# FFN weights laid out transposed by the host and made ternary in pieces of 512 columns; small inputs in one transfer

## The chip, the cores and the metric

The kernel runs on one NeuronCore of a Trainium2 chip, as one launch. The metric is device time in microseconds (us). Engines are TensorE (PE), VectorE (DVE), ScalarE (ACT), GpSimd (POOL) and SyncE (SP), which here issues all transfers. Each engine works off its own instructions in the order in which they are written; semaphores hold them to each other.

## What is computed

For 16 batches of 256 tokens of 512 elements: a gated attention (mLSTM, 8 heads of 64) on a layer norm of x with a context, then a gated FFN with quantised activations and ternary weights.

```python
def weight_quant(w):
    scale = 1.0 / jnp.clip(jnp.mean(jnp.abs(w)), EPS, None)
    q = jnp.clip(jnp.round(w * scale), -1.0, 1.0) / scale
    return w + jax.lax.stop_gradient(q - w)
def bitlinear(x, w):
    return act_quant(x) @ weight_quant(w).T
g = bitlinear(x, w_gate)                 # w_gate, w_up: (2048, 512)
u = bitlinear(x, w_up)
h = jnp.square(jax.nn.relu(g)) * u
return bitlinear(h, w_down)              # w_down: (512, 2048)
...
x = x + jnp.tanh(g_xattn[0]) * _L0_xattn_ref(_layernorm(x), ctx_1024, ctx_1024, ...)
x = x + jnp.tanh(g_ffn[0]) * _L0_ffn_ref(_layernorm(x), w_gate, w_up, w_down)
```

A weight becomes -1, 0 or 1 after division by the mean magnitude of its whole matrix; the mean must be known before any of it can be used.

## The kernel before

Tokens lie on the 128 partitions, two tiles (t = 0, 1) for a batch. `schedule` calls, on every engine, `step(b, n, m, par)`: the FFN of batch b, the attention of batch n and the preparation of batch m (layer norm, transposes, gates) in one hand-written order, with b = n - 1 and m = n + 1. The first calls are `step(None, None, 0, 0)`, `step(None, 0, 1, 1)` and `step(0, 1, 2, 0)`, which the code calls `first`, `second` and `third`; then a loop, and three closing steps.

Within a step TensorE multiplies the FFN's hidden layer in chunks of 512 columns (`chunk`, L1002, banks `gb` and `ub`), computes head scores (`scores`, L1033 and L1034), head outputs (`heads_out`, L1044 to L1046), gate products (`gate_products`, L1085), exponents (`exponents`, L1053) and the down projection (`down`, L1023). ScalarE takes the exponentials (L470, L471), relu and square (L435, L437), copies head outputs from the bank `tp` (`heads`, L479), and computes `lz` and `rz` (L557, L559), from which VectorE's `scale_heads` and the residual `x2` follow; GpSimd adds the second half, `x2[1]` (L395). `quantise_tokens` needs both. `gates_in` (L719) comes after it on VectorE, `running_max` (L739 to L750) gives `mparts`, which the next step's exponents need.

The weights are made ready in the first three steps. SyncE loads each in four pieces of 1 MB into `stage[0]` (gate, down) and `stage[1]` (up). `magnitudes(m, i)` sums absolute values (VectorE L618, ScalarE L415), `weight_total` adds them over partitions on TensorE (L974), and `weight_scale` makes mean and inverse (L608 to L613). Then, for each piece of 2048 elements a partition: `scale_weight` multiplies by the inverse and adds the magic number 12582912, which rounds (GpSimd L363, ScalarE L421); `round_weight` subtracts it into `rounded` in bf16 (VectorE L627, ScalarE L428); `weight_columns` transposes 16 blocks on TensorE into the banks `gb` and `ub` (L985); `weight_cols` copies two banks to `wgT`, `wuT` or `wdT` and clips to -1 and 1 (VectorE L642). The first `chunk` waits for all 24 banks (`wt_free`).

Eight small transfers bring gate kernels, biases and the two gates' scalars (`small_in`); ScalarE's first instruction and GpSimd's sum into `gk` (L357) wait for all of them. GpSimd builds constants first, `pick` among them (L351). `rounded`, `relu`, `h`, `ot`, `hqT` and `hq` share space: `relu` and `hq` lie in the `stage` tiles.

## Time and profile before

| | |
|---|---|
| median of 3 runs | 747.88 us (747.65 to 748.24) |
| span of the profiled execution | 748.3 us |
| TensorE busy | 676.4 us (90%) |
| VectorE busy | 604.8 us (81%) |
| ScalarE busy | 438.8 us (59%) |
| GpSimd busy | 122.7 us (16%) |
| memory traffic | 29.48 MB read, 8.39 MB written |
| chain that ended last | PE 60%, DVE 21%, issue 10%, ACT 6% |

In a table of stages the columns are the stage, its length, busy us of PE, PE weight load, DVE, ACT and POOL (with instructions), the granted clock, the DMA share and GB/s. A group by line ends in busy us, mean ns of one, and idle us before it. Times in a row count from the start of the span. "Idle before" names the time for which an engine had nothing running ahead of a group, and what ended it. The granted clock is given as a share of full speed: 1.00 is 2.4 GHz, 0.50 is 1.2 GHz.

### The profile page before, as it was taken

What the parts mean: (1) busy time and instruction counts of PE and PEld (TensorE: products, weight loads), DVE (VectorE), ACT (ScalarE), POOL (GpSimd) and SP (SyncE); (2) the same over time, 40 slices, a digit from 0 to 9 for tenths busy, and PEclk for the clock granted to TensorE, in tenths of its full rate; (3) what the DMA queues carried; (4) which work ended last, traced back from release to release, by engine and by line L of the source; (5) the groups of instructions that cost most, each with busy time, mean ns of one, the idle gap of its engine ahead of it and who ended that gap; (6) DMA issues with size and microseconds to landing.
All of it is one profiled execution on the core that took longest, in us unless ns stands there. A gap on an engine that the chain in (4) does not pass through costs nothing.

```text
span 748.3 us, 14597 instructions
## 1 busy us (share of the span) xinstructions
PE 676.4 (90%) x4634; PEld 460.8 (62%) x4710; DVE 604.8 (81%) x1374; ACT 438.8 (59%) x945; POOL 122.7 (16%) x188
## 2 busy tenths in 40 slices
PE   2778499999989999899989999899989999999896
PEld 2568467574756666575756666575757666675543
DVE  2585879797987979797987979797978979797966
ACT  2697556657574646656574646556574646566542
POOL 3341120202010110202020210202020200202000
PEclk9986699999999999999999999999999999999989
DMA  6950100102020201002020202002010102000000
GB/s 197 392 204 1 57 1 18 69 1 71 15 72 14 70 14 52 34 0 71 14 71 14 70 14 70 15 0 74 10 71 14 70 14 71 15 15 16 1 29 28
DMA packets 22132, 38.42 MB, mean 51 GB/s; under 512 B 5184, under 2 KB 5184, under 8 KB 21568
## 3 DMA queue, kind: packets, MB, share of 16 engines
q1 hardware_dynamic: 22080, 37.87, 14.2%
q14 instruction: 37, 0.30, 0.1%
q8 instruction: 15, 0.25, 0.1%
HBM read 29.48 MB, written 8.39 MB: 51 GB/s over the span
## 4 chain that ended last, share of the span: by engine, by line
PE 60%; DVE 21%; issue 10%; ACT 6%; DVEq 1%; DMA 1%; SPq 1%; POOL 0%; ACTq 0%
PE yb L1023 11%; PE ub L1002 11%; PE gb L1002 10%; PE ab L1033 5%; DVE hmaxes L657 4%; PE ab L1013 3%; PE tp L1044 3%; PE tp L1085 3%; PE tp L1046 2%; PE tp L1045 2%; PE ab L1053 2%; DVE dmat L763 2%; DVE stage L649 2%; PE ab L1034 2%; PE ab L1063 2%
## 5 line engine op out<-in xcount | busy, mean ns | idle before, releaser
L1002 PE MATMUL ub<-wuT,xqT 128*128 128x512 bf16 x497 | 131.7, 381 | 8.9 <-DVE stage L649 8.0
L1023 PE MATMUL yb<-wdT,stage 128*128 128x512 bf16 x483 | 133.6, 379 | 1.3 <-ACT stage L449 0.5
L1002 PE MATMUL gb<-wgT,xqT 128*128 128x512 bf16 x480 | 126.4, 383 | 5.9 <-ACT xqT L456 4.2
L479 ACT ACTIVATE ysb<-tp 128x260 f32<-128x260 f32 x64 | 24.7, 387 | 149.8 <-PE tp L1046 149.8
L379 POOL TENSOR_SCALAR_AFFINE_SELECT dmat<-dmat 128x256 f32<-128x256 f32 x128 | 61.8, 510 | 238.5 <-ACT dmat L471 238.3
L649 DVE TENSOR_TENSOR stage<-stage,ub 128x512 f32<-128x512 f32 x128 | 86.7, 680 | 16.5 <-ACT stage L437 16.5
L763 DVE SCALAR_TENSOR_TENSOR dmat<-ab,dmat 128x384 f32<-128x384 f32 x128 | 65.3, 551 | 40.0 <-PE ab L1034 39.3
L1002 PEld LDWEIGHTS ub<-wuT,xqT 128*128 128x128 bf16 x512 | 49.0, 98 | 68.2 <-DVE stage L649 9.8
L435 ACT ACTIVATE stage<-gb 128x512 f32<-128x512 f32 x128 | 76.5, 598 | 20.2 <-PE gb L1002 15.8
L437 ACT ACTIVATE stage<-stage 128x512 f32<-128x512 f32 x128 | 80.7, 630 | 4.1
L1023 PEld LDWEIGHTS yb<-wdT,stage 128*128 128x128 bf16 x512 | 59.3, 118 | 38.1 <-DVE stage L696 0.7
L657 DVE TENSOR_REDUCE hmaxes<-stage 128x1 f32<-128x1536 f32 (+1 forms) x64 | 77.6, 1213 | 0.6
L395 POOL TENSOR_TENSOR x<-ysq,xs 128x512 f32<-128x512 f32 x16 | 25.3, 1582 | 309.6 <-DVE ysq L796 309.6
L1002 PEld LDWEIGHTS gb<-wgT,xqT 128*128 128x128 bf16 x512 | 47.5, 101 | 44.7 <-issue 8.1
L470 ACT ACTIVATE dmat<-ab,a 128x256 f32<-128x256 f32 x128 | 62.3, 487 | 1.0 <-PE ab L1053 1.0
L1033 PE MATMUL ab<-qT,cT 64*128 64x256 f32 x256 | 55.0, 441 | 5.3 <-DVE dmat L763 5.2
L1044 PE MATMUL tp<-values,dmat 128*128 128x65 f32 x256 | 51.9, 285 | 5.7 <-issue 5.7
L1045 PE MATMUL tp<-values,dmat 128*128 128x65 f32 x256 | 50.5, 279 | 0.0
L1046 PE MATMUL tp<-values,dmat 128*128 128x65 f32 x256 | 50.5, 280 | 0.0
L471 ACT ACTIVATE dmat<-ab,a 128x128 f32<-128x128 f32 x128 | 49.6, 387 | 0.0
L679 DVE TENSOR_SCALAR stage<-stage,hqs 128x1024 f16<-128x1024 f32 x64 | 47.4, 783 | 2.4 <-DVE hqs L671 1.5
L1044 PEld LDWEIGHTS tp<-values,dmat 128*128 128x128 f32 x256 | 40.7, 194 | 13.6 <-issue 6.0
(134 smaller groups left out, 1198.4 us busy)
## 6 DMA issues: line engine op xcount, KB each, us to landing
xs<-in_x SPq DMA_DIRECT2D x16, 512.0 KB, 3.6
cx<-in_ctx SPq DMA_DIRECT2D x16, 512.0 KB, 4.4
out<-stage SPq DMA_DIRECT2D x32, 256.0 KB, 2.0
stage<-in_L_ffn_w_gate SPq DMA_DIRECT2D x4, 1024.0 KB, 11.1
stage<-in_L_ffn_w_up SPq DMA_DIRECT2D x4, 1024.0 KB, 13.9
stage<-in_L_ffn_w_down SPq DMA_DIRECT2D x4, 1024.0 KB, 5.4
gk<-in_L_xattn_igate_kernel SPq DMA_DIRECT2D x1, 48.0 KB, 4.4
gk<-in_L_xattn_fgate_kernel SPq DMA_DIRECT2D x1, 48.0 KB, 4.5
```

What stands on the lines that cost most here:

```text
L435: nc.scalar.activation(relu[:, c % 2, :], gb[c % 2][:, :], ACT.Relu).then_inc(g_free, 1)
L437: nc.scalar.activation(relu[:, c % 2, :], relu[:, c % 2, :], ACT.Square).then_inc(r2_ready, 1)
L470: nc.scalar.activation(dmat[:, hd, 0:2, :].rearrange("p c s -> p (c s)"), eb, ACT.Exp, bias=a[npar][:, 0, hd:hd + 1])
L649: nc.vector.tensor_tensor(h[t][:, c * CH:(c + 1) * CH], relu[:, c % 2, :], ub[c % 2][:, :], ALU.mult).then_inc(h_done, 1)
L657: nc.vector.tensor_reduce(hmaxes[:, t, part:part + 1], h[t][:, first * CH:last * CH], axis=AX_X, op=ALU.max, apply_absolute_value=True).th ...
L763: nc.vector.scalar_tensor_tensor(dh, ab[hd % 2][:, 0:3 * P], HD ** -0.5, dh, ALU.mult, ALU.mult).then_inc(a_free[hd % 2], 1)
L1002: last = nc.tensor.matmul(bank[c % 2][:, :], xqT[par][:, t, d, :], w[:, d, c * CH:(c + 1) * CH], start=(d == 0), stop=(d == KD - 1))
L1023: done = nc.tensor.matmul(yb[:, :], hqT[:, c, :], wdT[:, c, :], start=(c == 0), stop=(c == KF - 1))
L1033: nc.tensor.matmul(ab[e][:, 0:S], cT[npar][rows, kd, 0:P], qT[npar][rows, kd, 0:S], start=True, stop=True)
L1044: nc.tensor.matmul(o0, dmat[:, hd, 0, :], values[:, 0, hd, :], start=True, stop=True)
L1045: nc.tensor.matmul(o1, dmat[:, hd, 1, :], values[:, 0, hd, :], start=True, stop=False)
L1046: last = nc.tensor.matmul(o1, dmat[:, hd, 2, :], values[:, 1, hd, :], start=False, stop=True)
```

## The change

The host hands over `w_gate`, `w_up` and `w_down` transposed, so that they land in `stage` in the layout that the matmuls read, and packs gate kernels, biases and both scalars, the latter repeated for each partition, into one array of 128 x 226 floats. `weight_columns` (192 transposes), VectorE's `weight_cols` and the tiles `rounded` and `identb` go. A piece is now 512 columns of all four row blocks (gate, up) or four row blocks (down). After scaling with the magic number, gate and down pieces become ternary by ScalarE's Sign of the value less the magic number (`sign_weight`), up pieces by VectorE's subtract and max, then min (`round_weight`). The matmuls wait for the piece that they read (`w_ready`). `relu` and `hq` get tiles of their own. The work on `w_down` after its transfer (magnitudes, total, scaling, signs) moves from the second step to the third; `w_down`'s transfers wait for the signs of the gate pieces whose place they take. The order of other steps in `second` changes too: ScalarE takes all four exponentials at once, and batch 1's statistics and norm come after `normaliser`.

```diff
...
+        def weight_piece(m, i):
+            return stage[m % 2][:, PW * i:PW * (i + 1)]
+        def ternary_piece(m, i):
+            if m == 2:
+                return wdT[:, KD * i:KD * (i + 1), :]
+            return (wgT, wuT)[m][:, :, CH * i:CH * (i + 1)]
+        def by_rows(piece):
+            return piece.rearrange("p (k c) -> p k c", k=KD)
...
+            sp.dma_start(small[:, :], small_in).then_inc(small_ready, 16)
             sp.dma_start(xs[0][:, :, :], x[0].rearrange("(t p) d -> p t d", p=P)).then_inc(x_in[0], 16)
             sp.dma_start(cx[0][:, :, :], ctx_in[0].rearrange("(t p) d -> p t d", p=P)).then_inc(c_in[0], 16)
-            for i, (kern, bias) in enumerate(((wi, bi), (wf, bf))):
-                sp.dma_start(gk[:, :, i * NH:(i + 1) * NH], kern.rearrange("(c p) h -> p c h", p=P)).then_inc(small_in, 16)
...
-            def weights(m, w):
...
+            def weights(m, w, first, last):
+                wv = w.rearrange("(k p) f -> p k f", p=P)
+                for i in range(first, last):
                     if m == 2:
-                        sp.wait_ge(w_round[i % 2], i // 2 + 1)
-                    sp.dma_start(sv[:, rows * i:rows * (i + 1), :], wv[:, rows * i:rows * (i + 1), :]).then_inc(w_in[m][i], 16)
+                        sp.wait_ge(w_ready[0], i + 1)
+                        src = wv[:, KD * i:KD * (i + 1), :]
+                    else:
+                        src = wv[:, :, CH * i:CH * (i + 1)]
+                    sp.dma_start(by_rows(weight_piece(m, i)), src).then_inc(w_in[m][i], 16)
...
-            weights(0, w_gate)
+            weights(0, w_gate, 0, 4)
+            weights(1, w_up, 0, 2)
             load(1, 1)
-            weights(1, w_up)
-            weights(2, w_down)
+            weights(1, w_up, 2, 4)
+            weights(2, w_down, 0, 4)
...
                     gp.wait_ge(a_free[p % 2], exponent_use(n, p // 2) + 1)
...
+                    if b is None:
+                        scale_weight(0, p)
+                if at(b, 0):
+                    scale_weight(2, 0)
+                    scale_weight(2, 1)
                 if b is None:
                     scale_weight(1, 0)
-                    scale_weight(1, 2)
+                    scale_weight(1, 1)
...
                 if b is None:
-                    scale_weight(2, 0)
-                    scale_weight(2, 2)
+                    scale_weight(1, 2)
+                    scale_weight(1, 3)
...
-                nc.scalar.activation(x2[1][:, :, :].rearrange("p t d -> p (t d)").bitcast(BF16), stage[m % 2][:, PW * i:PW * (i + 1)],
-                                     ACT.Abs, accum_out=asum[:, m, i:i + 1]).then_inc(asum_done[1], 1)
+                nc.scalar.activation(wdT[:, 0:KD, :], by_rows(weight_piece(m, i)), ACT.Abs, accum_out=asum[:, m, i:i + 1]).then_inc(asum_done[1], 1)
...
+            def sign_weight(m, i, scaled):
+                act.wait_ge(w_scaled[m], scaled)
+                nc.scalar.activation(ternary_piece(m, i), by_rows(weight_piece(m, i)), ACT.Sign,
+                                     bias=minus_magic[:, :]).then_inc(w_ready[m], 1)
...
-                if third:
-                    round_weight(2, 3)
-                elif b is not None:
+                if b is not None and not third:
                     relu_square(b, 0, 0)
                 if n is not None:
                     exponentials(n, 0, npar)
                     exponentials(n, 1, npar)
-                if second:
...
-                if third:
+                if third or second:
                     exponentials(n, 2, npar)
                     exponentials(n, 3, npar)
+                if third:
                     relu_square(b, 0, 0)
                 if b is not None:
                     relu_square(b, 0, 1)
+                if third:
+                    magnitudes(2, 0, 4)
...
                     relu_square(b, 0, 2)
-                if n is not None and not third:
+                if third:
+                    magnitudes(2, 1, 5)
...
                 if second:
-                    scale_weight(0, 3)
-                    for i in range(4):
-                        magnitudes(1, i)
+                    sign_weight(0, 0, 1)
+                    magnitudes(1, 0, 2)
                 if first:
                     act.wait_ge(consts, 3)
-                if m is not None:
+                if m is not None and not second:
...
                     exp_minus_max(n, npar)
                     heads(n, 0)
-                if second:
-                    for i in range(4):
-                        magnitudes(2, i)
                 if b is not None:
                     relu_square(b, 0, 3)
+                if third:
+                    magnitudes(2, 2, 6)
+                    magnitudes(2, 3, 7)
...
                 if n is not None:
                     heads(n, 1)
                     if second:
-                        scale_weight(1, 1)
-                        round_weight(1, 1)
+                        sign_weight(0, 1, 2)
...
+                if third:
+                    scale_weight(2, 2)
+                    scale_weight(2, 3)
+                    sign_weight(2, 0, 4)
+                    sign_weight(2, 1, 4)
                 if b is not None:
                     relu_square(b, 1, 1)
                     hidden_cols(b, 0)
+                if third:
+                    sign_weight(2, 2, 4)
+                    sign_weight(2, 3, 4)
                 if second:
-                    for t in range(T):
-                        columns(m, 0, cT[par], t)
-                    scale_weight(1, 3)
+                    magnitudes(1, 2, 3)
+                    act.wait_ge(stat_step, STAT_K * m + 4)
+                    rstd_of(mv[:, :, 1], lnv[:, :], rstd[:, :], rstd_step, RSTD_K * m)
...
-                if m is not None and not second:
+                if second:
+                    sign_weight(0, 2, 3)
+                if m is not None:
...
+                if first:
+                    magnitudes(0, 2, 0)
                 if second:
-                    scale_weight(2, 3)
-                if first:
-                    magnitudes(0, 2)
-                    magnitudes(0, 3)
+                    sign_weight(0, 3, 4)
                 if n is not None:
                     tokens(n, npar)
-                if second:
-                    round_weight(2, 1)
...
+                if first:
+                    magnitudes(0, 3, 1)
...
+            def round_weight(i):
+                dve.wait_ge(w_scaled[1], i + 1)
+                nc.vector.tensor_scalar(ternary_piece(1, i), by_rows(weight_piece(1, i)), MAGIC32, -1.0,
+                                        ALU.subtract, ALU.max).then_inc(w_low, 1)
+                dve.wait_ge(w_low, i + 1)
+                nc.vector.tensor_scalar(ternary_piece(1, i), ternary_piece(1, i), 1.0, None, ALU.min).then_inc(w_ready[1], 1)
...
-                if m is not None:
+                if m is not None and not second:
                     attention_stats(m, par)
...
-                if second:
-                    round_weight(0, 0)
-                    round_weight(0, 1)
-                    weight_cols(0, 0)
...
                     if second:
-                        weight_cols(0, 2)
-                if m is not None:
+                        magnitudes(1, 1)
+                if m is not None and not second:
                     attention_norm(m, par)
...
+                if first:
+                    magnitudes(0, 0)
...
+                if n is not None:
+                    weigh(n, 6)
+                    weigh(n, 7)
+                    if at(b, 0):
+                        weight_scale(2)
+                        dve.wait_ge(winv_step, WINV[2])
+                        dve.wait_ge(tanh_done, 1)
+                        nc.vector.scalar_tensor_tensor(wprod[:, 2:3], wmean[:, 2:3], 1.0 / 127.0, tanhs[:, 1:2],
+                                                       ALU.mult, ALU.mult).then_inc(winv_step, 1)
+                if b is not None:
+                    quantise_hidden(b, 0, par)
+                    hidden(b, 1, 0)
+                if n is not None:
+                    normaliser(n, npar)
                 if second:
-                    weight_cols(0, 3)
+                    attention_stats(m, par)
+                    magnitudes(1, 3)
+                    attention_norm(m, par)
+                if b is not None:
+                    hidden_cols(b, 0)
...
+                if n is not None:
+                    if at(n, 0):
+                        dve.wait_ge(tanh_done, 1)
+                    scale_heads(n)
+                    residual(n, npar)
+                if second:
                     weight_scale(1)
                     dve.wait_ge(winv_step, WINV[1])
...
-                    normaliser(n, npar)
...
-                    weight_cols(1, 1)
-                    weight_scale(2)
...
+                if second:
+                    round_weight(0)
                 if m is not None:
-                    if second:
-                        weight_cols(1, 2)
                     log_forget(m)
                 if second:
-                    round_weight(2, 0)
+                    round_weight(1)
...
                 if first:
+                    magnitudes(0, 1)
                     weight_scale(0)
                 if second:
-                    weight_cols(1, 3)
-                    weight_cols(2, 0)
-                    round_weight(2, 2)
-                    weight_cols(2, 1)
-                    weight_cols(2, 2)
-                    weight_cols(2, 3)
+                    round_weight(2)
+                    round_weight(3)
...
-                pe.wait_ge(asum_done[1], 4 * m + 2)
+                pe.wait_ge(asum_done[0], (2, 4, 4)[m])
+                pe.wait_ge(asum_done[1], (2, 4, 8)[m])
...
-            def weight_columns(m, i, between=None):
...
-                        last = nc.tensor.transpose(wt_bank(g)[:, s * P:(s + 1) * P], rounded[:, i % 2, piece * P:(piece + 1) * P], identb[:, :])
...
+                for bank, w, full, free, ready in ((gb, wgT, g_full, g_free, w_ready[0]), (ub, wuT, u_full, h_done, w_ready[1]))[first:last]:
                     if at(b, 0) and t == 0:
-                        pe.wait_ge(wt_free, 24)
-                for bank, w, full, free in ((gb, wgT, g_full, g_free), (ub, wuT, u_full, h_done))[first:last]:
+                        pe.wait_ge(ready, c + 1)
...
+                    if at(b, 0) and t == 0 and c % KD == 0:
+                        pe.wait_ge(w_ready[2], c // KD + 1)
                     done = nc.tensor.matmul(yb[:, :], hqT[:, c, :], wdT[:, c, :], start=(c == 0), stop=(c == KF - 1))
...
                 if third:
-                    weight_columns(2, 2)
-                    weight_columns(2, 3)
                     exponents(n, 2, npar)
...
                     heads_out(n, 3, npar)
                 if second:
-                    weight_columns(1, 1)
+                    weight_total(1)
+                if third:
                     weight_total(2)
...
                 if first:
                     weight_total(0)
-                if second:
-                    weight_columns(1, 3)
-                    weight_columns(2, 0)
-                    weight_columns(2, 1)
...
+    laid = {name: np.asarray(a) for name, a in inputs.items()}
+    heads = laid["L0_xattn_igate_bias"].shape[0]
+    kernels = np.concatenate([laid["L0_xattn_igate_kernel"], laid["L0_xattn_fgate_kernel"]], axis=1)
+    kernels = kernels.reshape(-1, P, 2 * heads).transpose(1, 0, 2).reshape(P, -1)
+    biases = np.concatenate([laid["L0_xattn_igate_bias"], laid["L0_xattn_fgate_bias"]] * 2
+                            + [laid["g_xattn"], laid["g_ffn"]]).reshape(1, -1)
+    laid["small"] = np.concatenate([kernels, np.broadcast_to(biases, (P, biases.shape[1]))], axis=1)
+    for name in ("w_gate", "w_up", "w_down"):
+        laid[name] = laid["L0_ffn_" + name].T
...
```

## Rows read from the trace of the kernel before

**Rows 1.** Busy time by stage: window, each engine's busy us, clock, DMA.

```profile
100.00:120.00 20.00, 19.26 (x136) 13.93 (x137) 17.30 (x40) 9.87 (x22) 0.00 (x0) 1.00 0.00 1
...
131.20:172.00 40.80, 39.82 (x277) 26.94 (x282) 35.05 (x83) 24.26 (x57) 6.41 (x10) 1.00 0.10 36
```

**Rows 2.** Timelines of ScalarE: first exponential of batches 0, 1 and 2.

```profile
30.92 0.47 ACT L470 ACTIVATE dmat<-ab,a 128x256 f32<-128x256 f32 x1 [1.02 <-PE ab L1053]
...
92.83 0.46 ACT L470 ACTIVATE dmat<-ab,a 128x256 f32<-128x256 f32 x1
...
134.08 0.46 ACT L470 ACTIVATE dmat<-ab,a 128x256 f32<-128x256 f32 x1
```

**Rows 3.** Timeline of all engines, 0 to 24 us.

```profile
4.10 3.55 POOL L351 TENSOR_SCALAR_AFFINE_SELECT pick<-pick 72x1024 bf16<-72x1024 bf16 x3
...
12.93 0.20 ACT L406 ACTIVATE tanhs<-tanhs 128x2 f32<-128x2 f32 x1 [10.84 <-DMA tanhs<-in_g_ffn]
...
13.15 1.28 ACT L407 ACT_TABLE_LOAD   x1
...
15.60 1.86 PE L1085 MATMUL tp<-gk,cT 128*128 128x16 f32 x8 [8.01 <-ACT cT L441]
...
15.93 2.28 DVE L618 TENSOR_REDUCE asum<-stage 128x1 f32<-128x2048 f32 x1
```

**Rows 4.** Timeline, 22 to 60 us: gates, and the maximum's last part.

```profile
24.43 0.19 DVE L719 TENSOR_TENSOR gates<-tp,gbias 128x32 f32<-128x32 f32 x1 [3.75 <-PE tp L1085]
...
29.80 0.42 DVE L750 TENSOR_TENSOR mparts<-mres,mmid 8x256 bf16<-8x256 f32 x1
```

**Rows 5.** Same timeline: scores on TensorE, second head copy on ScalarE.

```profile
41.34 1.23 PE L1033 MATMUL ab<-qT,cT 64*128 64x256 f32 x4
...
56.83 0.37 ACT L479 ACTIVATE ysb<-tp 128x260 f32<-128x260 f32 x1
```

**Rows 6.** Timeline, 60 to 112 us: last head copy, `x2[1]`, scaling, gates.

```profile
64.40 0.39 ACT L479 ACTIVATE ysb<-tp 128x260 f32<-128x260 f32 x1 [3.09 <-PE tp L1046]
...
72.54 1.65 POOL L395 TENSOR_TENSOR x<-ysq,xs 128x512 f32<-128x512 f32 x1 [16.53 <-DVE ysq L796]
...
74.17 4.08 POOL L363 TENSOR_SCALAR stage<-stage,winv 128x2048 f32<-128x2048 f32 x2
...
81.59 0.19 DVE L719 TENSOR_TENSOR gates<-tp,gbias 128x32 f32<-128x32 f32 x1
```

**Rows 7.** Timeline of TensorE, 700 to 748.3 us: two of four groups.

```profile
711.20 1.89 PE L1002 MATMUL gb<-wgT,xqT 128*128 128x512 bf16 x4 [0.83 <-ACT xqT L456]
...
716.14 1.03 PE L1002 MATMUL ub<-wuT,xqT 128*128 128x512 bf16 x4
```

**Rows 8.** Groups by line and form, VectorE 90 and ScalarE 30.9 to 131.2.

```profile
L703 DVE BATCH_NORM_STATS2 st<-xs 128x6 f32<-128x512 f32 x2 | 1.3, 680 | 0.0
...
L713 DVE TENSOR_SCALAR q<-xs,mv,rstd 128x512 f32<-128x512 f32 x2 | 1.0, 538 | 0.0
...
L627 DVE TENSOR_SCALAR rounded<-stage 128x2048 bf16<-128x2048 f32 x1 | 1.2, 1215 | 0.0
...
L415 ACT ACTIVATE x<-stage 128x2048 bf16<-128x2048 f32 x8 | 15.4, 1923 | 0.5
...
L421 ACT ACTIVATE stage<-stage,winv 128x2048 f32<-128x2048 f32 x6 | 12.1, 2022 | 0.0
```

**Rows 9.** Timeline of ScalarE, 92 to 136 us: head copies and `lz`.

```profile
107.55 0.39 ACT L479 ACTIVATE ysb<-tp 128x260 f32<-128x260 f32 x1 [4.36 <-PE tp L1046]
...
109.83 0.39 ACT L479 ACTIVATE ysb<-tp 128x260 f32<-128x260 f32 x1 [0.74 <-PE tp L1046]
...
112.55 0.39 ACT L479 ACTIVATE ysb<-tp 128x260 f32<-128x260 f32 x1 [2.34 <-PE tp L1046]
...
115.56 0.39 ACT L479 ACTIVATE ysb<-tp 128x260 f32<-128x260 f32 x1 [0.89 <-PE tp L1046]
...
119.09 0.30 ACT L557 ACTIVATE lz<-zz,eps_rms 128x16 f32<-128x16 f32 x1
```

166 lines of the change are left out of this document (33 added, 133 removed).

## The prediction

> **What bounds the kernel now.** I read the page's shares first, then busy time by stage [rows 1]. In the steady loop TensorE works 39.8 us of every 40.8, and the diff leaves the loop's instructions alone; only the operands `hq` and `relu` move to tiles of their own. In the first 100 us no engine is full for long: a chain crosses from one to the next. So the change acts up to the start of batch 1's FFN (about 131 us), and what it shifts there is carried to the end one for one. I call the stretches A (up to ScalarE's first exponential, 30.9 us), B (to its exponentials of batch 1, 92.8) and C (to those of batch 2, 134.1) [rows 2]. The sum is made on the profiled span, 748.3 us, which is 0.4 above the median of 747.9.
>
> **A, the small inputs and the first step.** ScalarE waits 10.8 us for the last of eight small transfers and starts at 12.93; its table load and the columns follow, so the gate products start at 15.60 [rows 3]. Afterwards one transfer of 116 KB goes first and is not late. What is late next is GpSimd's selection into `pick` (ends 7.65 [rows 3]), then its identity copy and the sum into `gk` (0.3 each): products at 8.4, 7.2 us earlier. From there to the row maximum nothing changes: gates are read at 17.2 instead of 24.4, and the maximum is out at 23.0 instead of 30.2 [rows 4]. But `magnitudes(0, 1)` (2.3 us [rows 3]) now stands behind it on VectorE, and `weight_total(0)` on TensorE waits for that ahead of batch 0's exponents, where before it was long done. Exponentials start at 26.5: **A gains 4.4 us**. The weights' transfers start 5 us earlier.
>
> **B, what leaves.** Before the second head output is copied (56.8 [rows 5]) ScalarE works off four magnitudes in one run, and TensorE waits; a scaling and a rounding follow before the third; the last copy starts at 64.4 and ends at 64.8 [rows 6]. These leave or move to C, with 192 transposes on TensorE and all weight copies out of PSUM on VectorE. ScalarE keeps one sign and one magnitude before the first copy and one sign before the third; they lie in its waits. TensorE is late next: scores start when the last exponentials release their banks (31.5), the first head output at about 34.9, and four head outputs and two score pairs follow, TensorE alone. At the lower clock a head output takes 2.6 to 2.9 (ScalarE waits 3.1 for one after its previous copy [rows 6]) and a score pair 1.6 (1.2 by its larger halves [rows 5]); at the full one 1.5 and 0.9, by the ratio of the same four matmuls, 1.89 to 1.03 us [rows 7]. The last copy ends at 49.5 if the clock stays low, at 45.7 if it rises near 40 us. The transposes that filled TensorE here are gone, so I take the middle, 47.6: 17.2 us before 64.8, 4.4 of them from A.
>
> **B, what comes in.** From that copy to the end of GpSimd's `x2[1]` took 9.4 us [rows 6]. Afterwards, in VectorE's order: normaliser 2.4, the statistics of batch 1, 1.7, a magnitude 2.3, its norm 1.0 [rows 3, 8], head scaling and first residual 2.1, mean and inverse 0.6; then, ahead of `x2[1]` on GpSimd, `scale_weight(1, 0)` and `(1, 1)`, 3.9 (the pair took 4.1 beside VectorE [rows 6]); then 1.7. That is 15.7: x2 at 63.3. From x2 to the gates 7.4 again, since GpSimd again scales two pieces behind it while VectorE wants its own operations. Gates to row maximum take 5.8 [rows 4]; `round_weight(0)` adds one operation of 1.2 [rows 8] and an in-place minimum, which the trace does not show: between 0.2 (VectorE's shortest) and 1.2 (the same elements), I take 0.7, for half the bytes; the second rounding fills a wait for TensorE but for 0.1. So 7.8, and 0.6 to the exponentials: 79.1 instead of 92.8, where roundings stood between. **A and B together gain 13.7 us**, 11.8 to 15.6 by the clock in B.
> SyncE now holds `w_down`'s pieces behind four signs, and `load(2)` behind those. The last sign ends near 73; its piece is wanted 18 us into C, batch 2's statistics 8 us into C: covered. If the pieces came 20 us later, ScalarE would stop in C for the difference.
>
> **C, what is moved there.** All work on `w_down` moves here, nearly all to ScalarE: four magnitudes at 1.92 and a read of 0.2 each, 8.4; two scalings at 2.02, 4.0; four signs, unseen in the trace, between a magnitude's 1.92 and a scaling's 2.02 (which reads a scale tile), 7.8 [rows 8]. Overlaps taken off, 20.0 us, all before `lz` in ScalarE's order. Before, ScalarE idled between 92.8 and `lz` (119.1) in gaps of 4.4, 0.7, 2.3 and 0.9 us, 8.3 together [rows 2, 9]. Were all filled, C would grow by 11.7; were none, by 20.0. I place them. Two magnitudes (4.2) fit before the first head copy. The two others meet a gap of 0.7 and hold the second copy back 3.7 us; TensorE waits with the next head output; 0.6 comes back, so the fourth copy is 3.1 late. `weight_total(2)` needs all magnitudes and follows that output, so `quantise_hidden(0, 0)` on VectorE, with all behind it, waits some 8 us; ScalarE's queue hides that. Scalings and signs there, 11.8, meet no gap, for what could fill one stands behind them: `lz` is 14.7 late (3.1 + 11.8 less 0.2), and with it the head scaling, x2, and the next step.
> The clock comes on top. At the end of B TensorE is nearly idle, so C's first chunks start low. Near the end of the profile, after a pause, three groups of four matmuls took 1.7 to 1.9 us before one took 1.03 [rows 7]: for five or six such groups in C, less what ScalarE hides, 2.6 us. Between 20 and 28 us into C its pauses may lower it again: 0 to 4, I take 0, as they are shorter than B's. Ahead of the gate products TensorE is one third full while it waits for what follows `lz`: low again, over the first part of 7 us of dense work, 2.3. **C grows by 14.7 + 2.6 + 2.3 = 19.6 us**, bounds 11.7 and 24.
>
> **A rule against the change.** For 2048 elements a partition ScalarE takes 1.92 us and VectorE's rounding 1.22 [rows 8]. The Trainium skill, "ScalarE: Activation LUTs", "Rules for kernel authors", says to put maxima and minima on VectorE; by it, four signs of C would be some 3 us shorter there. The trace does not settle it, as VectorE is the fuller engine in C: 17.3 against 9.9 us of 20 [rows 1].
>
> **Sum.** 748.3 - 13.7 + 19.6 = 754.2 on the span, **753.8 us** on the median.
>
> **The rivals.**
> 1. *Even.* The clock rises soon in B and stays up in C: gain 15.6, C + 14.7 to 16.4: 747.0 to 748.7. For it: it rose within 5 us of chunk matmuls [rows 7]. Against: B and C have more pauses than before.
> 2. *Faster.* ScalarE's gaps take what I push behind them: C + 11.7, gain 13.7 to 15.6: 744.0 to 745.9. It decides if heads and chunks on TensorE run ahead of ScalarE's queue. For it: TensorE and VectorE lose their last weight work ahead of C's chunks. Against: the order puts 11.8 us in one run.
> 3. *Slower by table loads.* Sign may lie outside the loaded table set. Each group of signs between exponentials or logarithms then costs a load and one back, 1.28 us each [rows 3]. Three groups lie on the chain (two in B, one in C), 7.7 us: 761.5; it decides from the first sign. The Trainium skill, "ScalarE: Activation LUTs", "Table sets: the hidden batching unit", lists relu, copy, identity and abs as in every set and does not name sign there; it gives 2.66 us for a switch with its drain, by which this would be 770.
> 4. *Slower, the clock low throughout:* gain 11.8, C + 24: 760.1.
> That the transposes stay is excluded by the diff.
>
> **How the numbers follow.** My forecast 0.46, with its own range of 749.4 to 757; even 0.13; faster 0.25; table loads 0.05; clock low throughout 0.11. About 0.2% (1.5 us) is what a measurement can tell from no change. The forecast, the table loads and the low clock are slower, 0.62; faster 0.25; same 0.13. The range reaches through the faster case, with half a microsecond for rounding, to past the low clock: 743.5 to 761.0; the table loads and what I have not thought of stay out.
>
> **What would show it.** Gates read near 17 us; exponentials of batch 1 at 79 (77 to 81), of batch 2 at 140 (134 to 145); `lz` 41 to 46 us after the former; six scalings and signs on ScalarE with no gap but a relu between; VectorE waiting 8 us for the mean; a granted clock near half at the start of C. I am wrong if the two exponentials are under 54 us apart (ScalarE absorbed it), if the first comes after 82 (B is bound elsewhere), or if loop steps are no longer 41 us.

## The result, and the profile after

The change makes the kernel slower by half a per cent: 751.95 us (19 runs, 750.2 to 754.35) against 748.08 (19 runs), a ratio of 1.0046 [1.0034, 1.0058]. The forecast of 753.8 was 1.9 too high; "slower" was right. The agreement is in good part luck. I had 5.9 us for the stretches ahead of the loop. They cost 7.2 by the first profiles and 9.8 against the second profile of before (table below), and some 7 us that I had not seen at all came off the loop and the end. Half a microsecond of the difference lies outside the profiled span: a run's time is 1.5 us longer than its span in the kernel before and 2.0 in the kernel after.

The two profiled executions have the same span, 748.3 and 748.4 us, since the one of before lies nearly 2 us above a usual one and the one of after at the low end of its own. Stretches compare better than spans (in us; A, B and C are those of the prediction):

| stretch | before | before, second profile | after | change (first profile) | forecast |
|---|---|---|---|---|---|
| A, to batch 0's exponentials | 30.9 | 30.8 | 26.8 | -4.2 | -4.4 |
| B, to batch 1's | 61.9 | 59.4 | 54.6 | -7.3 | -9.3 |
| C, to batch 2's | 41.3 | 41.3 | 60.0 | +18.7 | +19.6 |
| the 13 steps from there to batch 15's exponentials | 541.8 | 542.0 | 535.6 | -6.1 | 0 |
| from there to the end | 72.5 | 72.6 | 71.5 | -1.0 | 0 |

Two of these changes are no firmer than the profiles that they come from. B gained 7.3 against the first profile of before and 4.8 against the second. The end took 70.1 to 72.7 in the fourteen profiles of this document's kernels, whatever was edited, so its 1.0 may be chance. C has the same weakness on the side of after: 60.0 here, but 62.1 and 62.9 in two more profiles of the same work (`after_padded` and `padded_13` below), with `lz` 45.7 and 45.4 us after the exponentials of batch 1 instead of 43.6. So a difference of 2 us in C or at `lz` between two single profiles shows nothing by itself.

ScalarE's timeline of the kernel after (columns: start, length, engine, line, operation, output and input, count, and the idle time before it with what ended it). It answers to [rows 2], [rows 6] and [rows 9]: exponentials of batches 0, 1 and 2, batch 0's four head copies and then batch 1's, and the work ahead of `lz`.

```profile
26.75 0.47 ACT L472 ACTIVATE dmat<-ab,a 128x256 f32<-128x256 f32 x1 [1.74 <-PE ab L1018]
...
38.61 0.39 ACT L481 ACTIVATE ysb<-tp 128x260 f32<-128x260 f32 x1 [2.89 <-PE tp L1011]
...
50.61 0.39 ACT L481 ACTIVATE ysb<-tp 128x260 f32<-128x260 f32 x1 [2.93 <-PE tp L1011]
...
81.35 0.47 ACT L472 ACTIVATE dmat<-ab,a 128x256 f32<-128x256 f32 x1 [1.02 <-PE ab L1018]
...
97.77 0.39 ACT L481 ACTIVATE ysb<-tp 128x260 f32<-128x260 f32 x1 [2.35 <-PE tp L1011]
...
103.20 0.37 ACT L481 ACTIVATE ysb<-tp 128x260 f32<-128x260 f32 x1
...
109.91 0.39 ACT L481 ACTIVATE ysb<-tp 128x260 f32<-128x260 f32 x1 [1.23 <-PE tp L1011]
...
111.39 3.88 ACT L424 ACTIVATE stage<-stage,winv 128x2048 f32<-128x2048 f32 x2
115.30 3.89 ACT L429 ACTIVATE wdT<-stage,minus_magic 128x2048 bf16<-128x2048 f32 x2
...
121.14 3.88 ACT L429 ACTIVATE wdT<-stage,minus_magic 128x2048 bf16<-128x2048 f32 x2
124.93 0.29 ACT L566 ACTIVATE lz<-zz,eps_rms 128x16 f32<-128x16 f32 x1
...
141.31 0.46 ACT L472 ACTIVATE dmat<-ab,a 128x256 f32<-128x256 f32 x1
```

The run of scalings and signs is as forecast, without a gap (relu, square and a copy stand between), and `lz` stands 43.6 us after the exponentials of batch 1; before it was 26.3 [rows 2, 9]. VectorE and TensorE in the same stretch of after:

```profile
110.08 0.16 DVE L614 TENSOR_REDUCE wmean<-yb 128x1 f32<-128x4 f32 x1 [8.16 <-PE yb L952]
...
84.41 1.91 PE L965 MATMUL gb<-wgT,xqT 128*128 128x512 bf16 x4
86.12 1.70 PE L965 MATMUL ub<-wuT,xqT 128*128 128x512 bf16 x4
87.65 1.03 PE L965 MATMUL gb<-wgT,xqT 128*128 128x512 bf16 x4
```

VectorE waits 8.16 us for the total of `w_down`'s magnitudes, the forecast 8. TensorE's first groups run at half speed, 1.91 and 1.70 against 1.03.

**The loop.** I had called it untouched. In the kernel before the steps are not equal: ScalarE's first exponentials come at 175.37, 216.55, 259.04, 300.20, 342.72, and so on to 593.69, steps of 41.2 and 42.5 in turn; five of 13 steps are 1.3 longer, each the one in which the loop jumps back. In the kernel after all 13 take 41.1 to 41.3. VectorE's timeline of the kernel before, at the first jump back:

```profile
219.25 0.20 DVE L680 TENSOR_SCALAR dq<-hm,wprod 128x1 f32<-128x1 f32 x1
220.91 1.28 DVE L649 TENSOR_TENSOR stage<-stage,ub 128x512 f32<-128x512 f32 x2 [1.46 <-ACT stage L437]
```

TensorE then waits for that, in the same kernel:

```profile
221.65 1.04 PE L1002 MATMUL ub<-wuT,xqT 128*128 128x512 bf16 x4 [1.50 <-DVE stage L649]
```

VectorE's row blames ScalarE, but the relu that it names ended at 216.64, 4.3 us before, and TensorE's matmuls into `ub` ended at 218.1: the data were there and VectorE did not start. The profile page's rows on the queues that fetch instructions move with it (packets, MB, share): `q14` does, `q8` hardly. Before:

```profile
q14 instruction: 37, 0.30, 0.1%
q8 instruction: 15, 0.25, 0.1%
```

After:

```profile
q8 instruction: 13, 0.21, 0.1%
q14 instruction: 11, 0.09, 0.0%
```

So two questions for the chip: what is C made of, and why did the loop become faster?

### The profile page after: what moved, and what is told of

Same layout as the page of the kernel before. It is cut to its first block, busy times and chain, and to the rows that moved or that the text cites. A ratio compares the mean times of both kernels' runs of the same rounds, so it can differ in the third digit from the quotient of the medians.

```text
span 748.4 us, 14246 instructions
## 1 busy us (share of the span) xinstructions
PE 681.9 (91%) x4518; PEld 456.9 (61%) x4518; DVE 593.8 (79%) x1352; ACT 434.5 (58%) x941; POOL 128.5 (17%) x192
## 4 chain that ended last, share of the span: by engine, by line
PE 59%; DVE 22%; issue 9%; ACT 7%; POOL 2%; DVEq 1%; POOLq 0%; ACTq 0%
PE yb L988 11%; PE gb L965 10%; PE ub L965 10%; PE ab L998 6%; DVE hmaxes L648 4%; PE ab L976 3%; PE tp L1009 3%; PE tp L1050 3%; PE tp L1011 3%; PE tp L1010 3%; PE ab L1018 2%; DVE dmat L753 2%; PE ab L999 2%; DVE stage L640 2%; ACT qT L443 2%
## 5 line engine op out<-in xcount | busy, mean ns | idle before, releaser
L988 PE MATMUL yb<-wdT,stage 128*128 128x512 bf16 x512 | 141.2, 382 | 0.5 <-ACT stage L451 0.5
L965 PE MATMUL gb<-wgT,xqT 128*128 128x512 bf16 x512 | 134.9, 387 | 4.6 <-ACT xqT L458 4.6
L965 PE MATMUL ub<-wuT,xqT 128*128 128x512 bf16 x512 | 133.4, 383 | 0.6 <-DVE stage L640 0.5
L640 DVE TENSOR_TENSOR stage<-relu,ub 128x512 f32<-128x512 f32 x128 | 87.0, 680 | 12.4 <-ACT relu L439 8.7
L437 ACT ACTIVATE relu<-gb 128x512 f32<-128x512 f32 x128 | 76.4, 597 | 18.5 <-PE gb L965 16.6
L439 ACT ACTIVATE relu<-relu 128x512 f32<-128x512 f32 x128 | 80.7, 630 | 4.0
L965 PEld LDWEIGHTS gb<-wgT,xqT 128*128 128x128 bf16 x512 | 48.1, 102 | 45.7 <-issue 9.4
L1009 PE MATMUL tp<-values,dmat 128*128 128x65 f32 x256 | 53.1, 290 | 2.9 <-issue 2.9
L1010 PE MATMUL tp<-values,dmat 128*128 128x65 f32 x256 | 51.7, 285 | 0.0
L1011 PE MATMUL tp<-values,dmat 128*128 128x65 f32 x256 | 51.7, 285 | 0.0
L669 DVE TENSOR_SCALAR hq<-stage,hqs 128x1024 f16<-128x1024 f32 x64 | 48.4, 798 | 1.1
L1009 PEld LDWEIGHTS tp<-values,dmat 128*128 128x128 f32 x256 | 41.5, 198 | 11.4 <-issue 3.9
```

Of the source, the lines that this page charges most:

```text
L437: nc.scalar.activation(relu[:, c % 2, :], gb[c % 2][:, :], ACT.Relu).then_inc(g_free, 1)
L439: nc.scalar.activation(relu[:, c % 2, :], relu[:, c % 2, :], ACT.Square).then_inc(r2_ready, 1)
L640: nc.vector.tensor_tensor(h[t][:, c * CH:(c + 1) * CH], relu[:, c % 2, :], ub[c % 2][:, :], ALU.mult).then_inc(h_done, 1)
L965: last = nc.tensor.matmul(bank[c % 2][:, :], xqT[par][:, t, d, :], w[:, d, c * CH:(c + 1) * CH], start=(d == 0), stop=(d == KD - 1))
L988: done = nc.tensor.matmul(yb[:, :], hqT[:, c, :], wdT[:, c, :], start=(c == 0), stop=(c == KF - 1))
L1009: nc.tensor.matmul(o0, dmat[:, hd, 0, :], values[:, 0, hd, :], start=True, stop=True)
```

## The experiments

### The kernel before once more, and the small inputs alone

`small_alone` is the kernel before with one packed transfer instead of eight, and nothing else of the change.

```diff
+            sp.dma_start(small[:, :], small_in).then_inc(small_ready, 16)
-            for i, (kern, bias) in enumerate(((wi, bi), (wf, bf))):
-                sp.dma_start(gk[:, :, i * NH:(i + 1) * NH], ...).then_inc(small_in, 16)
...
-            act.wait_ge(small_in, 16 * 8)
+            act.wait_ge(small_ready, 16)
```

Expected of the kernel before, of `small_alone`:

> The kernel before, unchanged. In its profile five of the loop's fourteen steps (each second one, where the loop jumps back) took 42.5 us instead of 41.2, with VectorE idle 1.5 us although ScalarE's relu that it is said to wait for had been done 4 us earlier. Theory L (the jump back costs VectorE an instruction fetch, a property of this program): the profile shows the same five steps of 42.4 to 42.6 us, total within 0.2% of before. Rival (a chance of one execution): some of the five, or none, are long, and total stays the same within 0.2%.

> The kernel before with the small inputs packed into one transfer that goes first, and nothing else. By the working of stretch A: gates read near 17.3 instead of 24.4 us, first exponential at 23.7 instead of 30.9, since the magnitudes stand where they stood. Theory 1 (the start is a chain, the rest of B moves with it): exponentials of batch 1 at 85.7, total 7.2 us shorter, 741. Rival (B is held by weights that come from memory, which move only 5 us earlier): exponentials of batch 1 at 88 to 92, total 743 to 748.

The second profile of before shows the same five long steps, so they belong to the kernel and not to one execution. B, however, was 59.4 instead of 61.9: its fourth head output took 2.02 of waiting where the first profile had 3.09 [rows 6], and what follows it another 1.5 less. `small_alone` took 742.11 us, ratio 0.9918 [0.9903, 0.9934], with exponentials at 24.2, 86.0 and 127.3 and the five long steps left. The transfer alone is worth 6 us, which A shows (-6.6); the rest of the change costs 9.8 us on top (742.1 to 751.95). In the changed kernel A gains only 4.2, because `weight_total(0)` waits on TensorE, ahead of the exponents, for a magnitude on VectorE, as forecast.

### GpSimd's x2[1] ahead of two scalings

```diff
-                if b is None:
-                    scale_weight(1, 0)
-                    scale_weight(1, 1)
...
                 nc.gpsimd.tensor_tensor(x2[npar][:, 1, :], ...)
                 if b is None:
+                    scale_weight(1, 0)
+                    scale_weight(1, 1)
```

> The changed kernel with GpSimd's second half of the residual of batch 0 ahead of the scalings of the up pieces 0 and 1 (all four scalings now follow it). Theory 1: x2[1] is on the chain of B, so the exponentials of batch 1 come 3.9 us earlier, 77.5 instead of 81.35, less up to 2 us by which VectorE's operations meet more of GpSimd's scalings; total 2 to 4 us below the changed kernel. Rival (the chain of B goes past x2[1], for example by the up pieces' rounding, which would now start later): exponentials of batch 1 at 81 or later, total the same or up to 2 us longer.

750.37 us, ratio to before 1.0018 [1.0004, 1.0032]; exponentials at 26.7, 79.2 and 141.1. B gains 2.2, as the theory has it. By these profiles C gives back 2.0 of it: ScalarE's second relu of C waited 2.15 for a chunk, where after waited 1.09 (88.71), and six of TensorE's chunk groups ran at the lower clock instead of five. But C's 62.0 is what other profiles of the changed kernel's C have too, and the medians do not lose it: the two ratios to before, 1.0046 and 1.0018, lie 2.1 us apart. So that the edit makes C longer is not shown.

```profile
87.60 0.60 ACT L436 ACTIVATE relu<-gb 128x512 f32<-128x512 f32 x1 [2.15 <-PE gb L964]
```

### Two of w_down's magnitudes on VectorE

```diff
                 if third:
-                    magnitudes(2, 2, 6)          # ScalarE
-                    magnitudes(2, 3, 7)
...
+                    magnitudes(2, 2)             # VectorE, behind the last weigh
+                    magnitudes(2, 3)
```

> The changed kernel with the magnitudes of down pieces 2 and 3 on VectorE (2.3 us each, ahead of the weighing of heads 6 and 7), where it idled 8 us before the mean, instead of on ScalarE. Theory 1 (ScalarE's queue sets stretch C): second head copy 4 us earlier, lz 3 to 4 us earlier (40 instead of 43.6 us after the exponentials of batch 1), less what VectorE's 4.6 us cost heads 6 and 7; total 1 to 4 us below the changed kernel. Rival (TensorE's low clock or VectorE sets C): lz moves by under 1 us, total the same or longer.

750.09 us, ratio 1.0029 [1.0012, 1.0046]. Batch 1's second and third head copies come at 100.6 and 103.3 instead of 103.2 and 105.7; `lz` comes 41.5 us after the exponentials instead of 43.6. Of 4.2 us taken from ScalarE 2.1 arrive at `lz`, by one profile each. The second head copy, 19.1 us after the exponentials instead of 21.9, says the same more firmly, since it came at 21.7 and 23.0 in the other profiles of after. In the total the gain is not clear of noise: the intervals of this kernel and of after overlap.

### TensorE kept busy in its waits

```diff
+            def warm(count, bank):
+                for _ in range(count):
+                    nc.tensor.matmul(bank[:, :], hot[:, 0:P], hot[:, :], start=True, stop=True)
```

The calls stand where the expectation lists them.

> The changed kernel with matmuls whose result nobody reads, 128x512 bf16 from a tile of zeros, in TensorE's waits up to batch 2: 8 before the first exponents, 2 behind these, 2 and 2 between head outputs, 20 before the cumulative sum and 8 behind it in the second step, then 8, 12 and 6 in the waits of the third. Theory (TensorE's low clock is a term of its own in B and C): the head outputs of batch 0 take 1.5 to 1.7 us instead of 2.6, the last head copy ends at 47 to 48.5 instead of 51.0, the first chunks of batch 0 take 1.03 from the first group on instead of 1.91, lz comes 1.5 to 3 us earlier after the exponentials of batch 1 (43.6), and the exponentials of batch 2 come 4 to 7 us earlier than at 141.3; time 745 to 748. Rival (ScalarE's queue hides the clock in C, and VectorE's and GpSimd's in B): the groups get shorter but lz stays at 43 or more and the time at 750 or above.

750.79 us, ratio 1.0054 [1.0027, 1.0081]: no gain, and both theories have a part. TensorE's timeline of this kernel, ahead of the head outputs of batch 0, at one of them, and ahead of C and at its first chunk:

```profile
21.33 3.62 PE L1091 MATMUL ub<-hot 128*128 128x512 bf16 x8
...
36.24 0.69 PE L1011 MATMUL tp<-values,dmat 128*128 128x65 f32 x2
...
70.19 6.24 PE L1091 MATMUL ub<-hot 128*128 128x512 bf16 x20
...
86.27 1.03 PE L967 MATMUL gb<-wgT,xqT 128*128 128x512 bf16 x4
```

In B eight extra matmuls took 3.62, 0.45 each, and the head outputs behind them stayed as slow as without (0.69 for the first two matmuls in both); the copies came 0.5 to 2.0 us later, by the extra work. In C, behind 20 that took 0.31 each on average and eight more, no chunk was slow any more: `lz` came 40.2 us after the exponentials instead of 43.6, the next exponentials 57.8 instead of 60.0. So the clock is worth 3.4 us at `lz` in C by these two profiles, where I had 2.6; against the two other profiles of after it is 5.1 and 5.5. A third of that is lost again behind `lz`, where I had put no extra work. B's part stays untested, for B did not become fast.

### Four edits at once

The gates' total behind the exponents; `x2[1]` first; two magnitudes on VectorE, all scalings of `w_down` on GpSimd, the last sign behind the context's columns; down's total ahead of a chunk.

```diff
+                if second:
+                    weight_total(0)              # TensorE, behind max_columns
...
-                    scale_weight(2, 2)           # ScalarE
-                    scale_weight(2, 3)
-                    sign_weight(2, 0, 4)
-                    sign_weight(2, 1, 4)
+                    sign_weight(2, 0, 1)
+                    sign_weight(2, 1, 2)
```

> The changed kernel with four edits: the sum of the gate weights' magnitudes behind the exponents of batch 0 on TensorE's queue instead of ahead of them (in A); x2[1] ahead of two scalings on GpSimd (in B); in C two magnitudes on VectorE instead of ScalarE, all four down scalings on GpSimd, and the four signs on ScalarE one by one, the last one behind the context columns; the weights' total of down ahead of the first chunk of the second half. Theory (ScalarE's run ahead of lz sets C): exponentials of batch 0 at 24.5 instead of 26.75, of batch 1 another 2.2 earlier at about 76.9; lz 35 to 38 us after them instead of 43.6; exponentials of batch 2 at 130 to 132; time 741 to 743. Rival (something else is late as soon as ScalarE is relieved, TensorE's low clock or GpSimd's scalings at 2 us each): lz at 39 or more after the exponentials of batch 1 and a time of 745 to 749. Loop steps stay at 41.2 by the theory on its position, with 228 instructions ahead of it.

742.88 us, ratio 0.9925 [0.9911, 0.994]: the time of the theory with the `lz` of the rival. A gains 1.8, B 2.2, C 4.0 (exponentials at 24.95, 77.39, 133.36), `lz` stands 39.6 behind. ScalarE was given back 10 us of C and used four. So the queue isn't the only thing that holds C.

The profile shows what these edits put in its place. `weight_total(2)` now stands ahead of the last head output on TensorE and waits there for VectorE's two magnitudes:

```profile
101.27 0.59 PE L950 MATMUL yb<-asum,ones 128*128 128x4 f32 x2 [2.58 <-DVE asum L619]
```

Behind that wait two chunk groups run at half speed (1.87 and 1.91), and the fourth head copy comes 30.4 us after the exponentials of batch 1, later than the 28.6 of after. The run ahead of `lz` is shorter by 5.8 us (9.2 from that copy instead of 15.0).

### w_down's scalings and signs cut to one column, then its magnitudes too

```diff
-                w = weight_piece(m, i)
+                w = weight_piece(m, i)[:, 0:1]                       # scale_weight on ScalarE
...
+                    nc.gpsimd.memset(wdT[:, KD:, :], 0.0)            # GpSimd, end of B
...
+                if m == 2:                                           # sign_weight; magnitudes the same
+                    nc.scalar.activation(wdT[:, KD * i, 0:1], weight_piece(m, i)[:, 0:1], ACT.Sign, ...)
+                    return
```

> The changed kernel with the two scalings of w_down on ScalarE and its four signs cut to one column of 2048 each, at the same places and with the same signals; GpSimd sets the rest of the tile to zero at the end of B. So w_down's ternary values are not made, and the output is not the reference's; the four magnitudes stay. Theory (11.8 us of ScalarE ahead of lz are what C pays for the move): the six take about 0.2 us each, lz comes 9.5 to 10.6 us earlier, 33 to 34 us after the exponentials of batch 1 instead of 43.6, the exponentials of batch 2 at 130 to 132 instead of 141.3, time 741 to 742.5. Rival (a second bound stands close behind ScalarE's queue: TensorE waiting for VectorE's hq and for the late total of magnitudes): lz 36 or more after the exponentials of batch 1, time 744 to 748. Loop steps 41.2 by both.

> signs_cut with the four magnitudes of w_down cut to one column as well (0.2 us each instead of 1.92), so that no work on w_down is left in C but its signals; the output is not the reference's. In signs_cut lz waited for VectorE, 38.1 us after the exponentials of batch 1, and VectorE had waited 8 us for the total behind the magnitudes. Theory (that late total is the second bound): without the magnitudes the second head copy comes 3.7 us earlier, the total 3 to 5 us earlier, VectorE's wait for it falls to 5 or less, lz comes 30 to 34 us after the exponentials of batch 1, and C takes 46 to 49 us instead of 53.4 (41.3 before the change, with 2.6 and 2.3 of the estimate for TensorE's low clock on top). Rival (the pauses of TensorE and its low clock make C long whatever ScalarE does): lz at 36 or more, C at 51 or more. B keeps the 5 us that setting w_down's tile to zero cost it in signs_cut; time about 744 by the theory, 748 by the rival.

`signs_cut`: 749.2 us, ratio 1.0012 [1.0, 1.0023]; `down_cut`: 746.09, ratio 0.9977 [0.9952, 1.0002]. Both lose 5.2 us in B to the setting of the tile, which the last section comes to; C begins 11 us after it has ended. `signs_cut` had `lz` at 38.1 and C at 53.4, the rival's figures; its time is above both forecasts, which left the 5.2 out. `down_cut` had 33.5 and 48.8, the theory's, but a time between theory and rival. So the queue is not all of C's price, but a wait behind it stands close. In `down_cut`, the total on VectorE and then `lz` on ScalarE:

```profile
111.13 0.16 DVE L623 TENSOR_REDUCE wmean<-yb 128x1 f32<-128x4 f32 x1 [4.04 <-PE yb L961]
...
120.01 0.31 ACT L575 ACTIVATE lz<-zz,eps_rms 128x16 f32<-128x16 f32 x1 [1.38 <-DVE zz L787]
```

That makes the ledger of C, by one profile each: 41.3 before; 48.8 with `w_down`'s signals and order but none of its work on ScalarE; 53.4 with the magnitudes; 60.0 with scalings and signs. By the medians the magnitudes are worth less than the ledger's 4.6 (3.1 us between the two kernels), and scalings and signs more than its 6.5 (2.8 us and the 5.2 lost in B make 8).

Contrary to what its expectation says, `down_cut` still has work on `w_down` in C: GpSimd's two scalings. `lz` stands 7.2 us later in it than before (33.5 against 26.3). 1.7 of that are there by the fourth head copy (24.5 us after the exponentials instead of 22.7 [rows 2, 9]), with two chunk groups at 1.91 and 1.71: the low clock. The other 5.5 were in no term of mine; `lz` follows that copy after 9.1 us, and before after 3.5 [rows 9]. The rows of VectorE say where they go. `weight_total(2)` stands behind the last head output on TensorE, so VectorE waits 4.0 us for it and makes mean and inverse (0.7) before it starts the hidden layer's quantisation. That is then slowed, beside GpSimd's scalings:

```profile
111.78 3.92 POOL L368 TENSOR_SCALAR stage<-stage,winv 128x2048 f32<-128x2048 f32 x2 [18.65 <-DVE winv L628]
...
112.51 1.25 DVE L664 TENSOR_TENSOR hmax<-hmaxes 128x1 f32<-128x1 f32 x1
...
114.49 2.41 DVE L678 TENSOR_SCALAR hq<-stage,hqs 128x1024 f16<-128x1024 f32 x2
```

The same two operations in the kernel before, with GpSimd idle:

```profile
112.33 0.16 DVE L664 TENSOR_TENSOR hmax<-hmaxes 128x1 f32<-128x1 f32 x1
...
113.22 1.42 DVE L679 TENSOR_SCALAR stage<-stage,hqs 128x1024 f16<-128x1024 f32 x2
```

These two make 2.1 us. 4.0, 0.7 and 2.1 are 6.8; 1.2 come off again, as before VectorE waited 0.6 for the last head copy and ScalarE was 0.6 late for `lz`. No kernel here takes the wait or the scalings away alone, so this split is read from rows and not tested.

### Where the loop's 6 us come from

VectorE's program before has 252 instructions ahead of the loop's body, waits counted, and after 226; the body has 334 in both. If the stall hangs on that, padding must bring it back or take it away. Four kernels differ from those that they are made of only by memsets of one element a partition on VectorE, ahead of everything, and the small tile that these write:

```diff
+            for i in range(26):          # or 13, or 77
+                nc.vector.memset(padding[:, i:i + 1], 0.0)
             schedule(dve, step)
```

> The changed kernel with 26 one-element memsets on VectorE ahead of everything, so that 252 instructions stand ahead of its loop's body on VectorE, as in the kernel before, instead of 226; the padding writes a tile that nobody reads and ends before the first input lands at 4.9 us. Theory (the gain of the loop comes from where the loop lies in VectorE's program, not from the work that was moved): the stall at the jump back returns, five steps of the loop take 42.4 to 42.6 us instead of 41.2, VectorE's row on the first relu after the jump has about 1.3 us of idle time before it, the queue that fetches instructions moves about 0.30 MB instead of 0.09, and the time rises by 5 to 6.5 us, to about 757.5. Rival (the stall depends on what the loop works on, the tiles of its own for hq and relu): all steps stay at 41.2 and the time is 752 within 1.5. Neither expects a difference ahead of the loop.

> The kernel before with the small inputs in one transfer (742.1 us when run alone) and 77 memsets of padding on VectorE ahead of everything, so that 329 instructions stand ahead of the loop's body and the loop of 334 ends at 663. Theory (position): five long steps of 42.5 turn into 41.2 and the time falls by 5 to 6.5 us, to about 736, less up to 0.5 us if the padding reaches past the first input at 4.9 us. Rival 1 (position matters, but this one is no better): still 742 within 1. Rival 2 (contents): 742 as well, and the padded changed kernel shows 752.

> The changed kernel with 13 memsets of padding on VectorE, 239 instructions ahead of its loop's body: half way between 226 (no stall) and 252 (a stall at every jump back). It is one look for where the border lies, seen in the loop's steps (41.2 or 42.5 us) and in the packets of the instruction queue (11 or 37). If the stall comes once the loop's last instructions lie past a fixed place, it is all or nothing: either all five jumps show it or none, and the border is in 240 to 252 or in 227 to 239. If it were a race between fetching and executing, some of the five jumps would show it and others not.

> The kernel before with nothing changed but 77 one-element memsets on VectorE ahead of everything, so that its loop's body begins at VectorE's instruction 329 instead of 252. Theory (position alone): the five long steps of 42.5 turn into 41.2, the instruction queue moves 12 packets instead of 37, nothing else moves, and the time falls by 6 to 7.5 us, to 741 to 742 (with the small inputs in one transfer the same padding gave 7.3 less, 734.8). Rival (the gain needs the earlier start of the weights, or is made ahead of the loop): under 4 us.

| kernel | instructions ahead | loop ends at | long steps | packets on q14 | time, us |
|---|---|---|---|---|---|
| before | 252 | 586 | 5 | 37 | 748.1 |
| before, padded by 77 | 329 | 663 | 0 | 12 | 742.3 |
| small inputs alone | 252 | 586 | 5 | 37 | 742.1 |
| the same, padded by 77 | 329 | 663 | 0 | 12 | 734.8 |
| after | 226 | 560 | 0 | 11 | 751.95 |
| after, padded by 13 | 239 | 573 | 0 | 11 | 753.7 (one run) |
| after, padded by 26 | 252 | 586 | 5 | 37 | 759.2 |

The ratios to before are 0.9914 [0.9888, 0.9941] for `before_padded`, 0.9819 [0.9799, 0.984] for `small_padded` and 1.0134 [1.0112, 1.0157] for `after_padded`. The stall follows the number: `small_alone`, with other tiles than the kernel before but 252 instructions, has it, and `relieved`, with 228, has not. The padding's tile takes some room too, but that would not explain the packets. VectorE in `after_padded`, at its first jump back:

```profile
228.74 0.20 DVE L671 TENSOR_SCALAR dq<-hm,wprod 128x1 f32<-128x1 f32 x1
230.38 1.28 DVE L641 TENSOR_TENSOR stage<-relu,ub 128x512 f32<-128x512 f32 x2 [1.44 <-ACT relu L440]
```

and the row of its profile page:

```profile
q14 instruction: 37, 0.30, 0.1%
```

So this is settled: the tiles of their own for `relu` and `hq` have nothing to do with it (the rival), and the changed kernel owes its 6 us to having 26 fewer VectorE instructions ahead of its loop. `after_padded` has that undone and is 7.2 slower; 6.7 of it lie in the loop. The kernel with 239 puts the border between 239 and 252. The Trainium skill ("Runtime: NRT & Kernel Launch", "Instruction fetch mechanics") says that a taken branch whose target is outside a window of two blocks must fetch it first; the five stalls and 26 more packets of 8 KB agree with that in kind. Its blocks of 256 instructions don't say which case stalls: counted from the program's start, loops from 226 to 560 and from 252 to 586 both touch three blocks, and only the second stalls.

`small_padded`, at 734.8 us, beats both kernels: 1.8% below before. It takes of the change only the one transfer. It is also the fair measure for the rest of the change: with no stall in either loop, the kernel after is 17.2 us slower, 18.7 of it in C.

## Why the prediction was right, and where it was not

- **A: right.** Gates read at 17.52 (17.2), exponentials at 26.75 (26.5); the magnitude ahead of the exponents took 2.29. `relieved` puts the price of its place at 1.8 us.
- **B, the head outputs: mis-sized.** I had 49.5 for the low clock and 45.7 for the high one, and took 47.6 because the transposes were gone. The last copy ended at 51.0, past even the low one: copies stand 4.3, 4.3 and 3.3 us apart, the first two times for a score pair and a head output at low speed, the last for a head output alone. That is 3.4 us too little: 1.9 is the middle that I took, 0.9 a later start of the first head output (35.75 instead of 34.9), and 0.5 a gap ahead of the last one.
- **B, behind them: right.** `x2[1]` was done 14.9 us after the last copy (15.7), gates were read 7.4 later (7.4), exponentials 8.1 after these (8.4). The in-place minimum took 0.71 us (0.7). So 81.35 against 79.1 is the head outputs, less a microsecond that the rest was too dear. What B gains, 7.3 or 4.8, hangs on the profile of before: my 92.8 came from the slower one.
- **C: the sum right (18.7 against 19.6), but not what its parts are worth.** The fourth head copy is 5.8 late (3.1 + 2.6), and the run behind it adds 11.5 (11.6): `lz` is 17.3 later, 14.7 + 2.6 to the digit. The digit is luck, as two more profiles have 19.1 and 19.5. I said that ScalarE's queue hides VectorE's wait of 8 us. It does, but what it hides is a second bound close behind, which would stand if the queue were empty: 5.4 us behind by these profiles, over 7 by the others. A reader of my sum would have promised 11.8 us for taking the scalings and signs away; it is 6.5 by the profiles and about 8 by the medians.
- **The clock in C: right in kind, perhaps too small** (3.4 to 5.5 us at `lz` by `kept_warm`, 2.6 by me). But the mark that I gave for it failed: the granted clock at the start of C did not show near half.

In the table of stages of after, the second row shows the clock's share, the first does not, though it holds the groups of 1.91 and 1.70:

```profile
84.00:88.00 4.00, 3.99 (x12) 1.67 (x13) 0.66 (x2) 3.59 (x10) 3.97 (x9) 1.00 0.01 2
102.00:110.00 8.00, 6.33 (x35) 4.59 (x36) 0.00 (x0) 3.27 (x7) 0.00 (x0) 0.79 0.01 2
```

- **Table loads for Sign: false.** The trace has two table loads, both before 4.6 us; eight signs ran at 2.02 and 1.99 us on average among exponentials and logarithms, without one. The groups of ScalarE by line:

```profile
L429 ACT ACTIVATE wgT<-stage,minus_magic 128x2048 bf16<-128x2048 f32 x4 | 8.1, 2020 | 0.0
L429 ACT ACTIVATE wdT<-stage,minus_magic 128x2048 bf16<-128x2048 f32 x4 | 7.8, 1992 | 0.0
L424 ACT ACTIVATE stage<-stage,winv 128x2048 f32<-128x2048 f32 x2 | 3.9, 1987 | 0.0
L411 ACT ACT_TABLE_LOAD x1 | 1.3, 1283 | 0.8 <-PEq L1191 0.8
L412 ACT ACT_TABLE_LOAD x1 | 1.3, 1283 | 0.0
```

- **Not in the prediction: the loop, -6.1 us, and the end, -1.0.** The step that failed is "the diff leaves the loop's instructions alone". It does, but it moves them. The signs were in the trace of before: steps of 41.2 and 42.5 in turn, and a VectorE row with 1.46 us of idle time put down to a relu 4 us old. I had read one step of the loop [rows 1] and taken it for all. Without this the changed kernel would stand at 759.2, as `after_padded` does, near the top of my range and 5.4 above my forecast. Nearly all of that is what the stretches ahead of the loop cost more than I had.

What stays open: why B in the kernel before takes 59.4 in some executions and 61.9 in others, why the end varies by 2.6, whether B's head outputs could run at the higher clock, how the 5.5 us of `down_cut` behind the fourth head copy divide between the late total and GpSimd's scalings, and what exactly sets the border between 239 and 252.

## What to carry to other kernels

Before calling a loop untouched, list the times of one event over all its steps: steps that alternate mean a stall at the jump back, and a few idle instructions ahead of the loop on that engine may remove it (here 6 us, where the whole change cost 4). Work that fits "under" a long queue should be priced by what stands second: cut the queue in an experiment, and the gain shows how near the next bound is. Moving the preparation of weights into a later step also moves the mean that everything there waits for, and puts GpSimd's scalings beside VectorE's work: together these held `lz` back 5.5 us with ScalarE relieved, nearly as much as the moved scalings and signs. And take more than one profile of either kernel before reading a difference of 2 us from a stretch.

## What the runs showed of the hardware

- **A jump back can stall VectorE by 1.3 us**, depending on where the loop lies in its program: 26 more instruction packets of 8 KB for five jumps, all five or none in every profile taken.
- **VectorE can be held up by GpSimd until GpSimd is through.** Two subtractions of 128x512 in f32 from and to SBUF took 0.85 us together in C of `signs_cut`, with GpSimd idle; in B of after, beside GpSimd's scaling, 3.36, and in `signs_cut`, beside the setting of `w_down`'s tile as well, 8.53. After, VectorE, then GpSimd:

```profile
66.84 3.36 DVE L809 TENSOR_SCALAR ysq<-x,mv 128x512 f32<-128x512 f32 x2
...
65.84 4.08 POOL L368 TENSOR_SCALAR stage<-stage,winv 128x2048 f32<-128x2048 f32 x2
```

`signs_cut`, the same two engines:

```profile
66.86 8.53 DVE L814 TENSOR_SCALAR ysq<-x,mv 128x512 f32<-128x512 f32 x2
...
69.89 5.21 POOL L404 MEMSET wdT<- 128x6144 bf16 x1
```

In both, VectorE ended 0.3 us after GpSimd (70.20 and 69.92; 75.39 and 75.10). The Trainium skill ("Advanced Engine Details and Errata", "VectorE Performance Modes") says that VectorE's second port to SBUF, the memory on the chip, is shared with GpSimd, whose instructions and VectorE's two-port ones block each other; the traces agree, as far as VectorE's work ends when GpSimd's does, but do not show the port.

- **The part of TensorE's work that runs at half speed moves by microseconds.** C of after took 60.0, 62.1 and 62.9 us in three profiles of the same program but for idle memsets ahead, with five, six and six groups of chunks at 1.4 us or more (the four matmuls of a group take 1.03 at full speed); the spread of the 19 runs of after, 4 us, would fit that, while the loop without stalls repeats to 0.1.
